# Two-term attention scores as row-group pairs: contraction of 32 partitions instead of 96 and 128, and three PSUM banks shared by maxima and turned results

## The reference

```python
proj = (ghs @ gru_W.T + gru_b).reshape(B, H, N, 2, 4).sum(-1)
gate_a, gate_b = sigmoid(proj)[..., 0:1], sigmoid(proj)[..., 1:2]
gate_out = gate_a * (gate_b * gru_const - 1.0) + 2.0
scores = einsum('bhid,bhjd->bhij', q, k) / sqrt(8) + gate_out * rel_embed[bucket(j - i)]
attn = softmax(scores, axis=-1)
out = einsum('bhij,bhjd->bhid', attn, v)   # then @ Wo.T + bo
```

## Time and profile before

| what | before |
|---|---|
| median of 3 runs | 2553.64 us |
| profiled execution, span (its own time is not listed apart) | 2551.5 us |
| first attention, first to last exponential started | 131.9 to 1181.2 us |
| TensorE busy over the span | 2283.1 us (89%) |
| VectorE busy | 1615.5 us (63%) |
| ScalarE busy | 1402.3 us (55%) |

### The profile page before, as it was taken

The page is one execution under the profiler, slowest core; times in us unless marked ns, Lnnn a source line. Parts: engine busy times, 40 slices in busy tenths (PEclk is TensorE's granted clock), DMA queues, the critical chain, the costliest instruction groups (busy, mean ns, idle before and its releaser), DMA issues. The chain is left out here.

```text
span 2551.5 us, 65137 instructions
## 1 busy us (share of the span) xinstructions
PE 2283.1 (89%) x22723; PEld 1399.8 (55%) x22723; DVE 1615.5 (63%) x3325; ACT 1402.3 (55%) x2072; POOL 991.0 (39%) x845
## 2 busy tenths in 40 slices
PE   5599999999999999998499977999899899899566
PEld 4355555555555555555355523767667667677345
DVE  5866666666666666666754586656556556564596
ACT  2245555555555555554222254888778788789221
POOL 0312222222222222231200013777767677778454
PEclk8799999999999999998699997999999999999797
DMA  5401110111111111100000053111111110110000
GB/s 137 124 21 27 26 25 24 24 26 26 26 26 26 24 23 26 26 20 10 1 1 0 1 192 121 39 31 35 37 29 39 27 39 26 30 36 2 1 13 21
DMA packets 108053, 88.66 MB, mean 35 GB/s; under 512 B 35732, under 2 KB 87556, under 8 KB 107916
## 3 DMA queue, kind: packets, MB, share of 16 engines
q1 hardware_dynamic: 105696, 84.22, 12.7%
q10 hardware_dynamic: 2220, 2.45, 0.4%
HBM read 58.12 MB, written 28.09 MB: 34 GB/s over the span
## 5 line engine op out<-in xcount | busy, mean ns | idle before, releaser
L923 DVE TENSOR_REDUCE b_mx<-psum 128x1 f32<-128x512 f32 x1024 | 659.6, 686 | 326.4 <-PE psum L794 164.6
L906 ACT ACTIVATE b_prob<-psum 128x1024 f32<-128x1024 f32 x512 | 524.5, 1024 | 463.3 <-PE psum L823 295.3
L1602 POOL TENSOR_TENSOR f_plo<-f_prob,f_phi 128x512 f16<-128x512 f32 x512 | 591.5, 1157 | 223.1 <-ACT f_phi L1728 192.3
L1744 DVE TENSOR_REDUCE f_mx<-psum 128x1 f32<-128x512 f32 x512 | 328.5, 683 | 224.8 <-PE psum L1633 223.8
L1727 ACT ACTIVATE f_prob<-psum,f_shift 128x512 f32<-128x512 f32 x512 | 353.1, 690 | 117.5 <-PE psum L1644 117.3
L1663 PE MATMUL psum<-f_vhi,f_plo 128*128 128x129 f16 x2048 | 377.2, 222 | 8.2 <-issue 8.2
L1659 PE MATMUL psum<-f_vhi,f_phi 128*128 128x129 f16 x2048 | 377.2, 222 | 0.6 <-POOL f_plo L1602 0.6
L1661 PE MATMUL psum<-f_vlo,f_phi 128*128 128x128 f16 x2048 | 376.9, 221 | 0.0
L1728 ACT ACTIVATE f_phi<-psum,f_shift 128x512 f16<-128x512 f32 x512 | 352.2, 688 | 0.0
L835 PE MATMUL psum<-b_prob,b_v 128*32 128x256 f32 x4096 | 327.2, 391 | 0.5 <-ACT b_prob L906 0.5
L753 POOL COPY b_v<-v 128x64 f32 x64 | 15.2, 238 | 776.0 <-PE psum L835 775.6
(11 more groups left out here) (298 smaller groups left out, 3570.7 us busy)
## 6 DMA issues: line engine op xcount, KB each, us to landing
d_qk<-e_qk SPq DMA_DIRECT2D x64, 256.0 KB, 2.6
b_toep<-d_line SPq DMA_DIRECT2D x128, 64.0 KB
f_qa<-d_qk SPq DMA_DIRECT2D x64, 128.0 KB, 2.9
f_ka<-d_qk SPq DMA_DIRECT2D x64, 128.0 KB, 3.0
d_q<-a_qk SPq DMA_DIRECT2D x16, 256.0 KB, 2.4
d_k<-a_qk SPq DMA_DIRECT2D x16, 256.0 KB, 2.6
b_q<-d_q SPq DMA_DIRECT2D x64, 64.0 KB
b_toep<-d_line SPq DMA_DIRECT2D x128, 32.0 KB
```

Source lines behind the costliest of these rows:

```text
L906: nc.scalar.activation(prob[:, t % 4, :].rearrange("p (a n) -> p a n", a=2), ps[:, EXP + 2 * (t % 2):EXP + 2 * (t % 2) + 2, :], ACT.Exp).t ...
L923: nc.vector.tensor_reduce(mx[:, b, t, half:half + 1], ps[:, MAX + half, :], AX.X, ALU.max).then_inc(s.max_read, 1)
L1602: nc.gpsimd.tensor_tensor(plo[:, t % 4, at], prob[:, t % 4, at], phi[:, t % 4, at], ALU.subtract).then_inc(s.plo_ready, 1)
L1744: nc.vector.tensor_reduce(mx[:, b, t, half:half + 1], ps[:, MAX + half, :], AX.X, ALU.max).then_inc(s.max_read, 1)
```

## The change

Contraction: q and k are stored in DRAM per head as 27 rows (8 features x 3 products of parts, and 3 rows of gate against far bias); the product of the two low parts is dropped. They are loaded into the 128 partitions four times, in groups of 32: partitions 0 to 31 and 32 to 63 serve the exponent's half 0 and half 1 (rows 27 and 28 of each group hold the maximum's two parts), 64 to 95 and 96 to 127 the maxima's half 0 and half 1. Each far matmul contracts one group of 32; the matmuls of half 0 and half 1 are issued alternately. The near matmuls are as before.

Order: in each step the maxima come first (far pair, near), then the exponent (far pair, near), then the values. `turn_m` is one f16 matmul of the maxima already split into parts by VectorE, and comes after tile 4. Banks 4 to 6 form a ring that maxima, turned output and turned maxima use in turn; the values move to bank 7.

DMAs: 16 loads per item for 10, 4 stores of maxima for 2, 11 stores per chunk in the projection for 6, 17 stores of tables for 5. The memories of k are filled with ones, those of q with zeros, with no second fill.

```diff
@@ phase_weights, SyncE
-                for x in range(2):
-                    for rows in (slice(0, 2), slice(2, 4)):
-                        sp.dma_start(g.d_far[x, :, rows, :], farw[:, x, :, :]).then_inc(tab_stored, 16)
+                for x in range(2):
+                    for b in range(B):
+                        tok = slice(b * N, (b + 1) * N)
+                        sp.dma_start(g.d_k[x, :, 3 * D0:3 * D0 + 2, tok], farw[:, x, 0:1, :].to_broadcast([H0, 2, N])).then_inc(tab_stored, 16)
+                        sp.dma_start(g.d_k[x, :, 3 * D0 + 2, tok], farw[:, x, 1, :]).then_inc(tab_stored, 16)
@@ phase_project0, SyncE
+                    for row, x in enumerate((hi, lo, hi)):
+                        sp.dma_start(head_rows(g.d_q, 0, row, at), x[:, 0, :]).then_inc(stored[u], 16)
+                    for side in range(2):
+                        for row, x in enumerate((hi, hi, lo)):
+                            sp.dma_start(head_rows(g.d_k, side * H0 * SCORE_ROWS * T, row, at), x[:, 1, :]).then_inc(stored[u], 16)
...
@@ phase_attend0
+        ring = []
+        for t in range(TB):
+            ring += [(t, 0), (t, 1)]
+            if t == OUT_STEP:
+                ring.append("o")
+            if t == M_STEP:
+                ring.append("m")
+        BANKS = 3
@@ load
+                    for half in range(2):
+                        mine, tok = slice(half * BANK, (half + 1) * BANK), bass.ds(b * N, N)
+                        part = bass.ds(b * N + half * BANK, BANK)
+                        for_exp, for_max = half * GROUP, (2 + half) * GROUP
+                        sp.dma_start(qs[b][for_max:for_max + M_ROW, :], one(g.d_q[head, :, tok])).then_inc(j, 16)
+                        sp.dma_start(qs[b][for_exp:for_exp + M_ROW, mine], one(g.d_q[head, :, part])).then_inc(j, 16)
+                        for side in range(2):
+                            sp.dma_start(ks[b][side][for_max:for_max + M_ROW, mine], one(g.d_k[side, head, :, part])).then_inc(j, 16)
+                            sp.dma_start(ks[b][side][for_exp:for_exp + M_ROW, :], one(g.d_k[side, head, :, tok])).then_inc(j, 16)
@@ TensorE
+                def bank_free(h, b, at):
+                    item = 4 * h + b
+                    at -= BANKS
...
+                        pe.wait_ge(s.max_read, done(min(unit, 2 * TB * NI - 1) if isinstance(unit, int) else unit))
+                def max_far(b, t, half, bank, right):
...
+                    x, y = (mid, c1) if right else (c0, mid)
...
+                    rows = slice((2 + half) * GROUP, (3 + half) * GROUP)
+                    return nc.tensor.matmul(ps[:, bank, x - c0:y - c0], qs[b][rows, t * P:(t + 1) * P], ks[b][int(right)][rows, x:y],
+                                            start=not (right and both), stop=not max_near_of(t, half), skip_group_check=True)
+                def maxima(b, t, banks):
+                    fars = [max_far(b, t, half, banks[half], right) for right in (False, True) for half in range(2)]
+                    for half in range(2):
+                        near = max_near(b, t, half, banks[half])
+                        (near or fars[2 + half] or fars[half]).then_inc(s.max_psum[half], 1)
+                def both_scores(h, b, t, ahead):
...
+                        for half in range(2):
+                            bank_free(h, b, at[half])
+                        maxima(bm, tm, [RING + x % BANKS for x in at])
+                    wait_exp(h, b, t)
+                    last = None
+                    for left in (False, True):
+                        for half in range(2):
+                            last = exp_far(b, t, half, left) or last
+                    for half in range(2):
+                        last = exp_near(b, t, half) or last
                     last.then_inc(s.exp_psum, 1)
...
@@ VectorE, join_max
+                    nc.vector.tensor_copy(mm[:, b % 2, :, 0, :], m).then_inc(s.m_hi, 1)
                     dve.wait_ge(s.m_hi, done(item))
+                    nc.vector.tensor_tensor(mm[:, b % 2, :, 1, :], m, mm[:, b % 2, :, 0, :], ALU.subtract).then_inc(s.m_lo, 1)
```

More of the change, by code:

```diff
@@ L638, in phase_attend0 @@
         LEAD = 12
[L639 to L640 removed]
+        M_ROW = SCORE_ROWS
+        GROUP = 32
         VW = 32
@@ new lines, in max_near_of, with max_near @@
+                def max_near_of(t, half):
+                    lo, hi = max(0, t * P - NEAR), min(N, (t + 1) * P + NEAR)
+                    n0, n1 = max(lo, half * BANK), min(hi, (half + 1) * BANK)
+                    return (n0, n1) if n1 > n0 else None
+                def max_near(b, t, half, bank):
+                    span = max_near_of(t, half)
+                    if span:
+                        n0, n1 = span
+                        u, c0 = n0 - (t - 1) * P, half * BANK
+                        return nc.tensor.matmul(ps[:, bank, n0 - c0:n1 - c0], diag[:, b, 0, t, :], toep[:, b, 0, u:u + n1 - n0],
+                                                start=False, stop=True, skip_group_check=True)
@@ L805, in score_exp, with exp_near_of @@
+                def exp_near_of(t, half):
                     near = []
@@ new lines, in exp_near_of, with exp_far @@
+                    return [x for x in near if half * BANK <= x[1] * P < (half + 1) * BANK]
+                def exp_far(b, t, half, left):
+                    bank = EXP + 2 * (t % 2) + half
+                    c0, c1 = half * BANK, (half + 1) * BANK
+                    mid = min(max(t * P, c0), c1)
+                    x, y = (mid, c1) if left else (c0, mid)
+                    if y <= x:
+                        return
+                    rows = slice(half * GROUP, (half + 1) * GROUP)
+                    both = c0 < mid < c1
+                    return nc.tensor.matmul(ps[:, bank, x - c0:y - c0], ks[b][int(not left)][rows, t * P:(t + 1) * P], qs[b][rows, x:y],
+                                            start=not (left and both), stop=not exp_near_of(t, half), skip_group_check=True)
@@ new lines, in exp_near @@
+                def exp_near(b, t, half):
+                    bank, c0 = EXP + 2 * (t % 2) + half, half * BANK
+                    last = None
+                    for blk, qt, x, y in exp_near_of(t, half):
+                        for tp, dp in ((0, 0), (0, 1), (1, 0)):
+                            at = qt * P - c0
+                            last = nc.tensor.matmul(ps[:, bank, at + x:at + y], toep[:, b, tp, blk * P:(blk + 1) * P], diag[:, b, dp, qt, x:y],
+                                                    start=False, stop=(tp, dp) == (1, 0), skip_group_check=True)
+                    return last
```

250 lines of the change are left out of this document (126 added, 124 removed).

## The result

| what | before | after |
|---|---|---|
| median (4 runs each, on one chip) | 2552.56 us | 3194.15 us |
| ratio, 95% interval | | 1.252 [1.250, 1.254] |
| profiled execution, its span | 2551.5 us | 3201.74, 3200.0 us |
| first to last exponential of the first attention | 131.9 to 1181.2 us | 148.3 to 1838.9 us |
| start to start of one tile, on average | 2.05 us | 3.31 us |

Slower by 25%, far outside the range of 2505 to 2635 us. Of the 648.5 us between the spans, 641.3 lie between the first and the last exponential (1690.6 for 1049.3 us), 16.4 ahead of them, and the rest of the program is 9.2 us shorter.

The account below looks back on a forecast made before the run. TensorE was taken to set the pace; -2.86 (pairs) + 0.16 (second starts) + 2.6 (division changes) = -0.10 us per item, x 64 = -6, + 8 outside = +2 on 2551.5: forecast 2556 us, range 2505 to 2635.

Parts of the forecast that it names:

- the sum: Whole kernel: -0.10 us per item, x 64 = -6 us, plus 8 us outside the loop: +2 us on 2551.5.
- a granted clock below 1.00 in the windows: Sign in the changed timeline that would make the forecast wrong; it had no size and no chance.
- Changes of division: TensorE in the loop: 26 more switches of the array's division per item at 0.10 us, 2.6 us slower.
- Rival 1: Loop: leaving the row groups is nearly free, step 1.85 us, 2505 us in all; chance 0.22.
- Pairs: Far matmuls in the loop: halves side by side, 9728 columns for 16384, 2.86 us gained per item, 0.16 lost to second starts.
- Rival 2: Loop: weight loads inside one row group are exposed, 0.10 us each, twelve per item, 2633 us in all; chance 0.16.
- Rival 3: Far matmuls in the loop: the halves do not run side by side at all, 2739 us in all; chance 0.05.
- Ring: TensorE's wait in the loop for VectorE to free a bank: taken as nothing, other end 0.2 us per item.
- Rival 4: Loop: ring or stores of the maxima become a wait of 1 us or so per item, 2620 us; chance 0.07.
- The sum of the loop: First attention's loop: -2.86 + 0.16 + 2.6 = -0.10 us per item, exponentials 2.04 us apart on average.
- Outside: Ahead of the loop: tables 3 us more, projection 2, start 3; together 8 us (6 to 10).
- said to be covered: SyncE's stores in the projection: earlier chunks come every 6.7 us and hide the 5.6 us of a chunk's stores.

Follow-up runs that it names:

- e14_pad: The changed kernel with 60 matmuls of 32 columns added ahead of the loop: 3170.84 us.
- e11_warm: The changed kernel with 60 whole-array matmuls of 512 columns (14.74 us of work) added ahead of the loop: 2529.01 us.
- e13_pause: e11_warm with one stop of TensorE after the first item, waiting for 16 fills of VectorE: 3186.27 us.
- e4_k64: The changed kernel with far matmuls over 64 rows, so the halves cannot run side by side; five changes of division per step stay: 3606.16 us.
- e5_order_near32: e1_order with the near matmuls on 32 rows, part of the bias product left out, five changes of division per step: 3128.04 us.
- e12_quad_lean: e3_quad without the bank waits that a later wait implies, run four times: median 2419.11 us.
- e15_warm: The same kernel as e11_warm, run four times: median 2528.87 us, 0.991 of before.
- e16_quad_pad: The kernel of e12_quad_lean with e14_pad's 60 tiny matmuls ahead of the loop: 2374.69 us, 0.930 of before.
- e1_order: The changed kernel's order, ring and split maxima, with far matmuls on 96 and 128 rows, operands and loads as before the change: 2587.76 us.
- e3_quad: The changed kernel with the far matmuls of maxima and exponent issued together in four row groups, then all near ones: 2466.99 us.

## Why the prediction was wrong, and where it was right

**The step that failed** is one that the sum never wrote down: every term was taken at the granted clock of 1.00 of the earlier trace rows, as if a busy TensorE had it. The prediction named "a granted clock below 1.00 in the windows" as what would make it wrong, gave that case no rival and no price, and read the 0.50 ahead of the loop as a matter of the load queue alone. What the runs put in its place: this loop has two lasting levels. Entered at 0.50 it stays there (`e14_pad`), entered at 1.00 it stays there (`e11_warm`), and one stop takes it from the upper to the lower for the rest of the loop (`e13_pause`). The loop before climbs by itself. By the spans, the changed kernel at the low clock is 3200.0 - 2527.2 = 672.8 us behind itself at the high one: the loop is 682.4 us longer (1690.6 for 1008.2), less the 12.0 us by which the added work delays the first exponential, and 2.4 us come behind it.

Which property makes the loop unable to climb is narrowed down, not settled. The loops that stayed low had five changes per step with either the far or the near matmuls on few rows (after, `e4_k64`, and `e5_order_near32` for some 900 us); with two or three changes all rose at least for a while; with six changes around whole-array streams it rose too. So neither reading alone holds. `e5_order_near32` left the low level at about 1043 us without any change in its work, and did so again within 17 us of the fall at its stop; what released it no run showed, and it shows that five changes do not hold the low level for certain. Among the changed kernel and the runs, only the changed kernel itself, `e12_quad_lean`, `e15_warm` and `e16_quad_pad` ran four times; how steady the clock of the others is from one execution to the next is not known. The Trainium skill (TensorE: Matmul & The Clock Gate, Part 1, "What's actually happening") has a throttled default that activity releases. The lift by dense work in `e11_warm` fits that: the clock reaches 1.00 within it. That an engine shown busy for 394 of 400 us was not released does not follow from it, so busy time in a profile is no promise of the clock.

**Point by point**, at the high clock, where the sum was meant to hold. TensorE in `e11_warm`, a step with two whole halves and one with a cut at 128 columns:

```profile
601.35 0.39 PE L834 MATMUL psum<-b_k1l,b_q 32*128 32x512 f16 x1
601.35 0.38 PE L834 MATMUL psum<-b_k1r,b_q 32*128 32x512 f16 x1
601.67 0.30 PE L848 MATMUL psum<-b_toep,b_diag 128*128 128x207 f16 x2
...
611.13 0.22 PE L834 MATMUL psum<-b_k2l,b_q 32*128 32x128 f16 x1
611.14 0.39 PE L834 MATMUL psum<-b_k2r,b_q 32*128 32x512 f16 x2
611.46 0.26 PE L848 MATMUL psum<-b_toep,b_diag 128*128 128x207 f16 x1
611.65 0.39 PE L870 MATMUL psum<-b_q,b_k0r 32*128 32x512 f16 x1
...
612.46 0.64 PE L928 MATMUL psum<-b_prob,b_v 128*32 128x256 f32 x8
612.91 0.22 PE L945 MATMUL psum<-b_ident,b_mm 128*16 128x128 f16 x1
...
613.42 0.28 PE L834 MATMUL psum<-b_k2l,b_q 32*128 32x256 f16 x1 [0.29 <-DVE b_mx L1031]
```

- **Changes of division: the price right, the count one per item too high.** 601.35 to 601.67 is 0.32 us for a pair of 512 columns: 0.22 and 0.10, as forecast. The near matmul of 207 columns takes 0.19 to the next pair (611.46 to 611.65). Rival 1 (leaving a group is free) is wrong. The Trainium skill (TensorEngine Tiling (Array Packing), "Key Properties") says that switching the mode drains TensorE; here that is 0.10 us. Behind the values `turn_m` costs no change of its own (0.45 us for the eight value matmuls, 612.46 to 612.91, where they take 0.57 with a change behind them), 0.12 us per item; the forecast counted 0.10 for it.
- **Pairs: the mechanism right, the gain sized 0.66 us per item too small.** The second start costs 0.01 us or less. But starts do not keep order across row groups. In the step at 611.13 the program has 128 columns of half 0, then 384 of half 0, then 512 of half 1. The 512 start with the 128 (611.14, a row that holds both later pieces), instead of behind the 384, and the near matmul starts 0.32 us later, as after two whole halves (601.35 to 601.67). Every pair costs 512 columns: 16 x 512 = 8192 per item, not 9728, and the 1536 columns between them are 0.66 us at the sum's 0.43 ns. The Trainium skill (TensorE: Matmul & The Clock Gate, "The mechanism") has matmuls start and end strictly in order; between row groups these rows show other starts.
- **Rival 2 is wrong.** Two pieces of 128 and 384 columns in one group are through in the same 0.32 us, and the second starts 0.07 us after the first, not 0.15, so its weight load is hidden. **Rival 3 is wrong**: the halves do run side by side.
- **Ring: slightly off.** Between 200 and 1000 us the first far matmuls of `e11_warm` waited 12.7 us for VectorE's reads of the maxima (3.7, 2.9, 3.7 and 2.4 in the four items of a loop iteration), 0.25 us for each of some 50 items, after `turn_m` (613.42); the far end was 0.2. Rival 4's place, then, at a quarter of its price.
- **The sum of the loop.** Forecast 2.04 us per step. With the pairs 0.66 / 8 = 0.08 us shorter, the change that `turn_m` doesn't cost another 0.02 and the ring's 0.03 on top it would have been 1.97 or 1.98, and 1.973 was measured. That the three corrections close the sum is arithmetic on these rows; no run took them apart. `e1_order`, the same order without pairs, stands at 2.13, its stops at the loop's head included.
- **Outside: 16.4 us instead of 8.** The timeline of SyncE in the changed kernel, its DMA issues, for the earlier trace rows:

```profile
33.50 0.42 SPq L212 DMA_DIRECT2D d_k<-w_farw  x1
...
90.19 2.13 SPq L431 DMA_DIRECT2D d_q<-a_qk  x3
92.42 4.04 SPq L434 DMA_DIRECT2D d_k<-a_qk  x6
...
97.82 1.86 SPq L431 DMA_DIRECT2D d_q<-a_qk  x3
...
115.51 0.35 SPq L740 DMA_DIRECT2D b_q<-d_q  x1
```

  The last of the 16 stores of tables is issued at 33.50, and VectorE begins the projection at 36.60 instead of 32.81: 3.8 us (forecast 3). The stores of a chunk take 7.6 us of SyncE (90.19 to 97.82), not 5.6: 0.67 to 0.71 us for one of q or k, where the rows had 0.39 and 0.54. That is more than the 6.7 us in which a chunk was made before, so SyncE, said to be covered, sets the pace of the projection: in the kernel before it waited for VectorE's parts in each of the 8 chunks, 33.5 us in all, and here once, 14.1 us, ahead of the first. The first load goes out at 115.51 instead of 102.62, 12.9 us later, of which the projection is 9.1 (forecast 2). From there to the first exponential it is 3.5 us more (forecast 3).
- **Behind the loop** the untouched rest takes 1361.1 us instead of 1370.3 in the changed kernel, 1358.1 in `e1_order`, but 1375.4 in `e3_quad`. The forecast had nothing there. The traces place most of the 9.2 us in the second attention, whose instructions are the same: there TensorE waits for nothing that is shown 16.2 us at L1643 and 8.2 us at L1663 in the kernel before (1550 to 2250 us), and 16.0 us and nothing at the same places (L1747, L1767) of the changed one (2208 to 2908 us). They look like the stops at the first loop's jump; no run tested it.

## What to carry to other kernels

Before a change to a TensorE-bound loop, read the granted clock ahead of the loop as well as in it, and ask what lifts it there: a loop of many short matmuls that switch the array's division may keep whichever level it is entered with, and here that was worth 665 us against an edit worth 23. If the clock of a busy loop is at 0.50, try a block of dense matmuls ahead of it and take stops out of it before touching its arithmetic. Each switch of the division costs 0.10 us here, so gather the matmuls of one division: four row groups in one run, with fewer waits and no stops at the jump, gave 7%, where pairs at the high clock gave 1%.

## What the runs showed of the hardware

- A loop can hold either of the two granted levels, 0.50 and 1.00, for over 1000 us with the same instructions (`e14_pad`, `e11_warm`), and a single stop of 10.82 us took one from the upper to the lower for the 1610 us that followed. `e5_order_near32` rose from the lower by itself, twice.
- Matmuls in different row groups overtake each other in their starts (611.14 in `e11_warm`); four start within 0.02 us (`e16_quad_pad`).
- An output of 16 columns after one of 32 (`turn_m` after the values) costs no change of division: 612.46 to 612.91 is 0.45 us for the eight value matmuls, 0.57 with the change behind them (614.78 to 615.35).
- TensorE stops for 2 to 5 us at the loop's jump in some kernels and executions, with 56 to 121 instruction packets between 200 and 1000 us, and never or once or twice in others, with 1 to 21. With 120 more instructions ahead of the loop, 60 matmuls and their weight loads, it went away in every kernel that had them; `e14_pad` is 23 us below the changed kernel, from which it differs in these 60 matmuls alone. The Trainium skill (Runtime: NRT & Kernel Launch, "Instruction fetch mechanics") says that a branch out of the fetched pages forces a fetch, which fits the packets. Why the place of the loop decides is open.
